# Attention phase of a two-layer gated cross-attention stack: weight codes made in the middle batches and read back in the last one

## The reference

```python
x = x + tanh(g_xattn[0]) * mha(layernorm(x), ctx, ctx, W_Q, b_Q, W_K, b_K, W_V, b_V, W_O, b_O)   # 16 heads of 32
x = x + tanh(g_ffn[0]) * bitlinear_ffn(layernorm(x), w_gate, w_up, w_down)    # inner width 2048
x = x + tanh(g_xattn[1]) * softmax_attention(layernorm(x), ctx)
x = x + tanh(g_ffn[1]) * (mxfp4(x, delta_act) @ mxfp4(weight, delta_w).T + bias)
# batch 8, 512 rows, width 512

def _weight_quant(w):                       # for w_gate, w_up, w_down
    scale = 1.0 / clip(mean(abs(w)), 1e-05)
    return clip(round(w * scale), -1.0, 1.0) / scale

def mxfp4(x, delta):                        # for the last weight, in blocks of 32
    scale = exp2(floor(log2(max(abs(x)))) - 2) * exp2(0.5 * tanh(4 * delta))
    return scale * sign(x) * fp4_round(clip(abs(x / scale), 0, 6))
```

## Time and profile before

| | us |
|---|---|
| median of 3 runs (lowest, highest) | 1665.71 (1661.42, 1668.95) |
| the profiled execution, its whole time | 1667.24 |
| its span, first to last instruction | 1665.5 |
| attention phase in it | 0 to about 891 |
| first exponential of the last batch | 760.2 |
| store of the last head group | 888.2 |
| mean granted TensorE clock, as a share of 2.4 GHz | 0.939 |

### The profile page before, as it was taken

How to read it: one execution, slowest core, us unless ns; L and a number is a source line. 1 busy time by engine, 2 the same in 40 slices (tenths; PEclk the granted TensorE clock), 3 DMA queues, 4 the chain that set the end, 5 groups by cost and what they waited for, 6 DMA issues and landing times. The chain is left out here.

```text
span 1665.5 us, 24701 instructions
## 1 busy us (share of the span) xinstructions
PE 1482.8 (89%) x6969; PEld 937.8 (56%) x6969; DVE 1237.6 (74%) x2141; ACT 875.0 (53%) x1434; POOL 922.8 (55%) x1160
## 2 busy tenths in 40 slices
PE   5799999899999999998654999999999838999996
PEld 3556556566655656665222555555555416888885
DVE  3567787978878777776653888888888707899996
ACT  4256566555555655645452555555555415555652
POOL 3167567567667657665473343344333115888874
PEclk9899999999999999998756999999999959999998
DMA  5836658394674838359654444444444362555531
GB/s 179 254 114 205 192 165 240 116 266 133 187 224 142 257 97 250 116 151 261 183 168 114 99 105 108 116 104 117 110 104 107 71 239 84 161 160 189 179 92 61
DMA packets 247452, 259.03 MB, mean 156 GB/s; under 512 B 140076, under 2 KB 156984, under 8 KB 243768
## 3 DMA queue, kind: packets, MB, share of 16 engines
q1 hardware_dynamic: 247352, 257.85, 53.9%
HBM read 149.50 MB, written 76.58 MB: 136 GB/s over the span
## 5 line engine op out<-in xcount | busy, mean ns | idle before, releaser
L660 ACT ACTIVATE a_probs<-a_sc 128x512 f32<-128x512 f32 x512 | 299.8, 595 | 298.5 <-PE a_sc L556 297.1
L745 DVE TENSOR_REDUCE a_negmax<-a_mx 128x1 f32<-128x512 f32 x512 | 337.6, 674 | 99.3 <-PE a_mx L539 98.3
L870 POOL TENSOR_TENSOR a_acc<-a_acc,a_probs 128x512 f32<-128x512 f32 x256 | 331.2, 1321 | 23.2 <-ACT a_probs L660 22.2
L870 POOL TENSOR_TENSOR a_acc<-a_probs 128x512 f32<-128x512 f32 x128 | 166.3, 1318 | 258.2 <-ACT a_probs L660 257.3
L539 PE MATMUL a_mx<-a_stack 96*128 96x512 f32 x512 | 230.8, 451 | 51.0 <-DVE a_negmax L745 38.7
L556 PE MATMUL a_sc<-a_stack 97*128 97x512 f32 x512 | 218.3, 429 | 26.7 <-ACT a_probs L660 19.2
L1020 PE MATMUL bank<-wcode,b_xq 128*128 128x512 bf16 x1024 | 228.0, 381 | 6.6 <-DMA b_xq<-b_xcode 6.6
L539 PEld LDWEIGHTS a_mx<-a_stack 96*128 96x128 f32 x512 | 101.8, 199 | 127.1 <-DVE a_negmax L745 76.4
L1020 PEld LDWEIGHTS bank<-wcode,b_xq 128*128 128x128 bf16 x1024 | 100.4, 98 | 129.2 <-DMA b_xq<-b_xcode 7.8
L751 DVE RECIPROCAL a_attn<-a_den 128x128 f32<-128x128 f32 x128 | 120.9, 948 | 59.7 <-PE a_den L584 59.7
L514 PE MATMUL a_work<-a_xt,k_wbuf 128*128 128x512 f32 x384 | 124.4, 439 | 13.0 <-DVE a_xt L722 13.0
(11 more groups left out here) (165 smaller groups left out, 2645.7 us busy)
## 6 DMA issues: line engine op xcount, KB each, us to landing
a_stack<-spill SPq DMA_DIRECT2D x192, 256.0 KB, 4.7
spill<-k_part SPq DMA_DIRECT2D x64, 512.0 KB, 3.5
ctx_t<-k_wo SPq DMA_DIRECT2D x16, 1024.0 KB, 7.9
c_ct<-ctx_t SPq DMA_DIRECT2D x7, 2048.0 KB, 8.2
a_stage<-in_x_dram SPq DMA_DIRECT2D x32, 256.0 KB, 5.0
a_stage<-in_ctx_dram SPq DMA_DIRECT2D x32, 256.0 KB, 2.7
attn_t<-a_attn SPq DMA_DIRECT2D x32, 256.0 KB, 4.4
b_xin<-in_x_dram SPq DMA_DIRECT2D x32, 256.0 KB, 2.7
```

Of the source, the lines that this page charges most:

```text
L660: nc.scalar.activation(probs[:, k, j, :], sc[i % 2][:], ACT.Exp, scale=SCALE).then_inc(exp_done, 1)
L745: nc.vector.tensor_reduce(negmax[:, g % 2, j, t:t + 1], mx[i % 2][:], axis=AX.X, op=ALU.max, negate=True).then_inc(mx_done, 1)
L870: nc.gpsimd.tensor_tensor(acc[:, j], probs[:, 0, j] if k == 1 else acc[:, j], probs[:, k, j], ALU.add)\
```

## The change

Three things move, all in `attention_phase`.

1. The last weight. It is loaded whole (1 MB) into `wsum` at the start, and its chain runs on VectorE in batch 0: steps 0 to 2 behind the last context transpose, steps 3 to 5 behind the second Q product's remainder, and four rounds of steps 6 to 11 between the first 20 `max` steps. One store writes it out. Batches 1 to 4 have no part of it any more.
2. The ternary weights. The sums are taken in 12 units of 128x2048 (two halves each) in groups 1 to 12, counted over all batches. From group 14 on, which is group 2 of batch 3, to group 25 (group 1 of batch 6), one unit a group is loaded, rounded in two halves (`uround`), clipped (`uclip`, `ucode`) and stored as codes to DRAM (`code_t`). The last batch only issues the twelve transposing DMAs, now from DRAM, and splits W_O.
3. The last batch's `pv` steps stand at ticks 74, 88, 112 and 142 (`pv_last`) in place of 128 to 149.

```diff
-    CH, SUMS, RAWS = 4, 8, 3
+    CH = 4
+    UNITS = 3 * CH
...
+    SUM_FIRST, CODE_FIRST, QSTEPS = 1, 14, 6 + 6 * C
...
-        raws = [nc.alloc_sbuf_tensor_at(f"raw{n}", [P, 2048], F32, offset=place["xt"] + 8192 * n)[:] for n in range(2)] + [wsum[:]]
-        codes = nc.alloc_sbuf_tensor_at("codes", [P, 2, 2048], BF16, offset=place["stage"])[:]
-        wraw, wmag = wsum[:, 1024:1024 + D], wsum[:, 1024 + D:1024 + 2 * D]
+        codes = nc.alloc_sbuf_tensor_at("codes", [P, 4, 1024], BF16, offset=place["wsum"])[:, :, 0:512]
+        wmag = probs[:, T - 1].rearrange("p j s -> p (j s)")
+
+        def unit(k):
+            per = wsrc[k // CH].shape[1] // CH
+            return per, wsrc[k // CH][:, k % CH * per:(k % CH + 1) * per, :]
...
-            ck.add(base + 20, 9, "sload", g)
-            ck.add(base + BURST + 2, 9, "sum", g)
-        ck.add(BURST + at["den"], 9, "wscale")
-        ck.add(-60, 9, "wload1")
-        for n in range(QSTEPS):
-            ck.add(PERIOD * (n // 6) + BURST + n % 6, 9, "wquant", n)
-        ck.add(2 * PERIOD + 30, 9, "wstore1")
-        for k, tick in enumerate(ITEM_AT):
-            ck.add(tick, 9, "rload", k)
-            for h in range(2):
-                ck.add(tick + 30 + 6 * h, 9, "rround", k, h)
-            ck.add(tick + 40, 9, "rclip", k)
-            ck.add(tick + 44, 9, "rcode", k)
-            ck.add(tick + 50, 9, "rturn", k)
+            ck.add(base + 60, 9, "uload", g)
+            ck.add(base + BURST + 2, 9, "sum", g, 0)
+            ck.add(base + BURST + 10, 9, "sum", g, 1)
+            ck.add(base + BURST + 2, 9, "uround", g, 0)
+            ck.add(base + BURST + 10, 9, "uround", g, 1)
+            ck.add(base + BURST + 12, 9, "uclip", g, 0)
+            ck.add(base + BURST + 20, 9, "uclip", g, 1)
+            ck.add(base + BURST + 29, 9, "ucode", g)
+            ck.add(base + BURST + 44, 9, "ustore", g)
+            for n, tick in enumerate((5, 35, 95)):
+                ck.add(base + tick, 9, "uturn", g, n)
+            for k, tick in enumerate((74, 88, 112, BURST + 14)):
+                ck.add(base + tick, 6, "pv_last", g, k)
+        ck.add(PERIOD + BURST + at["den"], 9, "wscale")
+        ck.add(PERIOD + 60, 9, "woload")
+        ck.add(PERIOD + BURST + 2, 9, "wohigh")
+        ck.add(PERIOD + BURST + 20, 9, "wolow")
...
                             load_small()
+                            sp.dma_start(wsum[:].rearrange("p (c e) -> p c e", c=C), weight.rearrange("(c p) e -> p c e", p=P))\
+                                .then_inc(q_loaded, 16)
...
+                    elif name == "uload":
+                        n = b * G + args[0]
+                        if n == SUM_FIRST:
+                            sp.wait_ge(q_step, QSTEPS)
+                            sp.dma_start(w1_code, wsum[:].rearrange("p (c e) -> p c e", c=C)).then_inc(q_stored, 16)
+                            sp.wait_ge(q_stored, 16)
+                        if SUM_FIRST <= n < SUM_FIRST + UNITS:
+                            k = n - SUM_FIRST
+                            if k:
+                                sp.wait_ge(summed, 2 * k)
+                            per, src = unit(k)
+                            sp.dma_start(wsum[:].rearrange("p (o i) -> p o i", o=per), src).then_inc(s_loaded, 16)
+                        if CODE_FIRST <= n < CODE_FIRST + UNITS:
+                            k = n - CODE_FIRST
+                            if k:
+                                sp.wait_ge(u_stored, 16 * k)
+                            else:
+                                sp.wait_ge(summed, 2 * UNITS)
+                            per, src = unit(k)
+                            sp.dma_start(wsum[:].rearrange("p (o i) -> p o i", o=per), src).then_inc(u_loaded, 16)
+                    elif name == "ustore" and CODE_FIRST <= b * G + args[0] < CODE_FIRST + UNITS:
+                        k = b * G + args[0] - CODE_FIRST
+                        sp.wait_ge(u_code, k + 1)
+                        sp.dma_start(code_t[k].rearrange("p (a n) -> p a n", a=4), codes).then_inc(u_stored, 16)
+                    elif name == "uturn" and b == NB - 1:
+                        k = args[0] * 3 + args[1]
                         if k == 0:
+                            sp.wait_ge(u_stored, 16 * UNITS)
                             sp.wait_ge(qk_full, 2 * G * NB)
+                        if k == 2 * CH:
                             sp.wait_ge(v_full, T * NB)
+                        sp.dma_start_transpose(wcode[:, k], code_t[k]).then_inc(u_turned, 16)
+                    elif name == "woload" and b == NB - 1:
+                        sp.wait_ge(u_stored, 16 * UNITS)
+                        sp.dma_start(wsum[:].rearrange("p (c e) -> p c e", c=C), w_o.rearrange("(c p) e -> p c e", p=P))\
+                            .then_inc(wo_loaded, 16)
...
-                    elif name == "pv":
+                    elif name in ("pv", "pv_last"):
                         g, k = args
+                        if (it + shift == NB - 1) != (name == "pv_last"):
+                            return
...
+                            if it + shift == 0 and g == 0 and k == T - 1:
+                                act.wait_ge(q_step, QSTEPS)
...
+                    elif name == "uround" and CODE_FIRST <= (it + shift) * G + args[0] < CODE_FIRST + UNITS:
+                        g, h = args
+                        k = (it + shift) * G + g - CODE_FIRST
+                        half = wsum[:, h * 1024:(h + 1) * 1024]
+                        if h == 0:
+                            act.wait_ge(u_loaded, 16 * (k + 1))
+                            if k == 0:
                                 act.wait_ge(w_scaled, 1)
+                        nc.scalar.activation(half, half, ACT.Copy, scale=scale_w[:, k // CH:k // CH + 1], bias=ROUND).then_inc(u_round, 1)
...
+                def quantise(n):
+                    c, step = (n - 6) // 6, n if n < 6 else 6 + (n - 6) % 6
+                    u, m = wsum[:], wmag
+                    if n >= 6:
+                        u, m = u[:, c * D:(c + 1) * D], m[:, c * D:(c + 1) * D]
+                    if n:
+                        dve.wait_ge(q_step, n)
...
+                        if it + shift == 0 and i == 2 * T - 1:
+                            dve.wait_ge(q_loaded, 16)
+                            for n in range(3):
+                                quantise(n)
...
+                        if it + shift == 0 and (g, side) == (1, Q):
+                            dve.wait_ge(exp2_done, 2)
+                            dve.wait_ge(gated, 1)
+                            for n in range(3, 6):
+                                quantise(n)
...
+                        slot_n = g * T * J + i - 1
+                        if it + shift == 0 and 0 <= slot_n < 5 * C:
+                            if slot_n % 5 == 0:
+                                quantise(6 + slot_n // 5 * 6)
+                            quantise(6 + slot_n // 5 * 6 + 1 + slot_n % 5)
...
+                    elif name == "uclip" and CODE_FIRST <= (it + shift) * G + args[0] < CODE_FIRST + UNITS:
+                        g, h = args
+                        k = (it + shift) * G + g - CODE_FIRST
+                        half = slice(h * 1024, (h + 1) * 1024)
+                        dve.wait_ge(u_round, 2 * k + h + 1)
+                        if h:
+                            dve.wait_ge(u_clip, 2 * k + 1)
+                        nc.vector.tensor_scalar(codes[:, 2 * h:2 * h + 2], wsum[:, half].rearrange("p (a n) -> p a n", a=2), ROUND, 1.0, ALU.subtract, ALU.min).then_inc(u_clip, 1)
+                    elif name == "ucode" and CODE_FIRST <= (it + shift) * G + args[0] < CODE_FIRST + UNITS:
+                        k = (it + shift) * G + args[0] - CODE_FIRST
+                        dve.wait_ge(u_clip, 2 * k + 2)
+                        nc.vector.tensor_scalar(codes, codes, -1.0, None, ALU.max).then_inc(u_code, 1)```

PE, last batch, group 2. `a_mx` and `a_sc` are the max and score products, `a_pvb` the V products, `a_den` first the turned maxima, then the sums. Before:

```order
L539 MATMUL a_mx<-a_stack 128x512 [waits a_mx_done]
L556 MATMUL a_sc<-a_stack 128x512 [waits a_exp_done] x3
L545 MATMUL a_den<-k_ident,a_negmax 16x128 [waits a_recip_done,a_mx_done]
L556 MATMUL a_sc<-a_stack 128x512 [waits a_exp_done]
L567 MATMUL a_pvb<-a_probs,a_v 32x512 [waits a_attn_done]
L567 MATMUL a_pvb<-a_probs,a_v 32x512 x11
L567 MATMUL a_pvb<-a_probs,a_v 32x512 [waits a_exp_done]
L567 MATMUL a_pvb<-a_probs,a_v 32x512 x3
L584 MATMUL a_den<-a_acc,a_ones 32x512 [waits a_mt_done,a_acc_done]
```

216 lines of the change are left out of this document (67 added, 149 removed).

## The result

| | before | after |
|---|---|---|
| median, us (7 runs each, side by side) | 1665.72 | 1677.88 |
| lowest, highest | 1661.42, 1668.95 | 1668.62, 1683.38 |
| ratio, 95% interval | | 1.0075 (1.0055 to 1.0094) |
| first exponential of all | 75.1 | 76.1 |
| first exponential of the last batch | 760.2 | 805.4 |

What follows compares the result with a forecast made beforehand. PE paces the middle batches; in the last, engines queue behind code items. Terms 7 + 2 - 7 + 3 + 6 - 30 = -19 took 1667.2 to 1648.2 profiled, 1647 as a median; range 1630 to 1664.

Steps and rivals of the forecast that it cites:

- Term E: Middle batches: a 1 MB load between spill and refill costs 1 us in six batches; +6 us, bounds 0 and +15.
- rival (3): 1 MB loads in 24 of 32 groups each delay something PE waits for; with 1.7 us each, 1682; chance with neighbours 0.09.
- F: Last batch: code items leave, POOL's sums are late next; 95.9 us against 128.0, -30 us, bounds -22 and -36.
- The V products: Last batch: moving them is worth little by itself; they fill PE's gaps and keep its clock up; no separate size.
- C: Third groups of batches 1 to 4: the last weight's chain leaves; -7 us, bounds -5 and -8.
- A: Batch 0: the last weight's chain comes in, steps 6 to 11 delay the last maximum; +7 us, bounds 0 and +12.
- B: Rest of batch 0: fourth round beside first scores, SP waiting for the weight's store, late first load; +2 us, bounds 0 and 3.
- D: Twelve middle groups: coding's rounding and clips in the burst cost 0.25 us a group; +3 us, bounds 0 and 12.
- Rival (1): The middle pays nothing: clips sit in the gap, refill not later; D = E = 0, A = 5, 1636; chance 0.17.
- signs of being wrong: Prediction wrong if middle batches grow by over 2 us each, or a last-batch group takes more than 26 us.

Runs made afterwards that it cites:

- late_g2: The changed kernel with the whole 1 MB load of each group 2 at tick 95, behind the refill, nothing split; one run, 1658.11 us.
- before_mrow: The kernel before with only the refill (2, K) moved to slot 47.5, so the row of maxima is issued ahead of it; 1656.71 us, ratio 0.9956.
- split_g2: The changed kernel with group 2's 1 MB load in halves, one before the spill (tick 45), one behind the refill (tick 95); 1653.88 us, ratio 0.9948.
- best: The changed kernel with group 2's load in halves (ticks 45, 95), refill (2, K) at slot 47.5, last batch's V products at old ticks; 1620.76 us, ratio 0.9751.
- best_nochain: As best, with the 24 steps 6 to 11 of the last weight's chain left out; 1618.75 us, ratio 0.9725.

## Why the prediction was wrong

**Term E is the step that failed**: "at some 300 GB/s the load takes 3.5 us, of which about 2.5 pass while SP waits for the spill. I take 1 us times 6". Measured it is some 47 us in place of 6 (of which about 1 is coding): 16 of wait and 12 of lower clock in third groups, and 19 in fourth ones. It failed in two places.

- The third groups. I let 2.5 of the 3.5 us pass unseen and put the bound at 2.5 a batch. The rows show 3.58 us of idle PE at 349.83 and up to 4.8, and the group grew by 3.7 to 6.9 in five batches and by 1.9 in the last. The load is not over when SP issues the refill; it lands 4.1 us later. And I put the clock at nothing here: in the five batches it fell to 0.88 to 0.94 in this group, and PE's own products took 1.5 to 2.9 us longer. The Trainium skill (DMA: Bandwidth & Descriptors, "Queues, rings and completion order") says that a DMA engine consumes descriptors in ring order, though a later one may finish its write first. The trace agrees with the order: the refill landed later with the load ahead of it, and the same load behind the refill (late_g2) cost under 0.3 us in five of the six batches. I had weighed that rule and set it aside for a guess about what passes during SP's wait, which no row of before could bear out.
- The fourth groups. The prediction had nothing for them ("refills of groups 1 to 3 show no wait on PE"). That sentence was true of the kernel before, and it looked at the wrong client. What waits there is not the refill but the row of maxima, one place behind it in SP's list. The rows were before me: the row made at 65.44 and issued at 70.26. I read them as slack ("SP had 4 us of slack"), when they were 5 us on the path at the start, as before_mrow shows; in the middle batches the same order was slack of about 2 us, and the loads used it up.

This is rival (3)'s mechanism, "the 1 MB loads", to which I gave 0.09. Its price was right in the mean and wrong in shape: 47 / 24 is 2.0 us a load where I had 1.7 for the slower case, but 12 of the 24 loads, in first and second groups, showed no wait of this kind, and 12 cost 3.9 each.

**F, the last batch: right in its number, in part by luck.** -32.9 against -30. With the V products at their old ticks F is -38, and moving them, which I put at almost nothing, cost 5: two misses of opposite sign. By groups 24.2, 23.1, 23.1 and 25.5 were worked out and 25.8, 22.3, 21.9 and 25.1 measured. That POOL's sums are late next holds as far as `den` stands right behind about 15 us of them; but they are not all that sets the end, since the batch changed by 5 us with the order of PE alone. The transposes from DRAM landed in 5.2 us in the middle where those from SBUF had taken 4.3, and no group of the last batch shows it.

**The V products: wrong sign.** "worth little by themselves", and "they fill PE's gaps and keep its clock up". The clock rose in the second group, and 5 us were lost. F without them is -38, beyond the bound of -36.

**C, the chain leaves: right.** Third groups of batches 1 and 2 are 23.6 and 23.5 us in split_g2 and 23.4 and 23.5 in best; 23.7 was forecast.

**A, the chain in batch 0: too large.** First exponential forecast at 82, measured 76.1. The last maximum of the first group did slip, from 64.1 to 68.5, near the +6 that I worked out; but of these 4.4 us the first exponential shows 1.0, or 1.4 to 2.2 if counted from the first maximum in the six kernels with this start, since SP issued the row only at 71.28 in after and at 70.26 before. With SP's stop gone the chain costs 2.5 (best_nochain). **B** can't be told from the rest.

**D, the coding: right within its bounds.** In best third groups without coding (batches 0 to 2) take 23.4 to 23.5 us and those with it (3 to 5) 23.6, 24.0 and 23.6; fourth groups 24.1 to 24.2 (batches 1 and 2) and 24.2. That is 0.3 and less than 0.1 us a group, and 0.25 was the term. The cost lies elsewhere, in first groups: those of batches 1 to 3 take 23.2 to 23.3 us and those of batches 4 and 5, with coding, 25.1 and 24.9, all at a clock of 1.00. In batch 5 of best the clips stand ahead of the first maximum of the group, which starts at 559.12, and a max product waits for it:

```profile
556.15 1.46 DVE L828 TENSOR_SCALAR codes<-a_wsum 128x1024 bf16<-128x1024 f32 x2
557.64 0.69 DVE L832 TENSOR_SCALAR codes<-codes 128x2048 bf16<-128x2048 bf16 x1
```

```profile
559.80 0.50 PE L546 MATMUL a_mx<-a_stack 96*128 96x512 f32 x1 [1.36 <-DVE a_negmax L788]
```

With 0.5 for batch 6 (24.3 against 23.8 before) that makes D about 5 where I had 3. No run left the coding out, so this is read from the rows and not tested. Second groups vary too much with the clock to tell. The prediction compared two different steps, 1505 ns while POOL adds and 410 when it is done. The same step tells the same: the chain's first clip of 512 columns, 1505 ns before, takes 419 ns in batch 0 after, where POOL is busy for a small part of the time. Twelve POOL additions of 1.3 us would be 15.6, not the +12 of the prediction. Rival (1), that the middle pays nothing, holds neither for D nor for E.

With E at zero the forecast would have been 1641. Best, where E is repaired, stands at 1620.76. Of the 20 us between, 8 are F's (-38 against -30) and 9 the first exponential (72.6 against 82), half of which was free in the kernel before. The upper bounds of the terms add up to +15, not to the +20 of the prediction; the measured +12 lies below both, with E alone at three times its bound. One of its signs of being wrong did show: middle batches were to grow by no more than 2 us, and batches 0 to 5 grew by 4.5 to 10.7 each.

## What to carry to other kernels

A bulk load should not stand in a queue between two DMAs of which the second is waited for: look for each transfer that an engine waits for and put the load behind it. A sequencer that waits for a landing holds back every DMA that stands behind it, so look what else is ready at that time, and let it go first. And a row that is "ready but issued 5 us later" is slack only if nobody waits for it; follow it to its reader before you call it so.

## What the runs showed of the hardware

- A refill of three DMAs of 256 KB was usable 5.2 us after its issue with no load ahead of it, and 7.5 us after it with 1 MB issued 3.0 us ahead. A load of 0.5 MB in the same place lengthened the group by 0.3 to 0.5 us in batches 0 to 2 (no coding), 1 MB by 3.7 to 5.5, of which 2.2 to 2.8 are idle time and the rest is a clock of 0.94 and 0.88.
- Moving one DMA issue by one place in SP's list gave the kernel before 7 us (0.9956, 0.9938 to 0.9974).
- Twelve V products moved in between the scores of each group of the last batch made it 5 us longer, in six kernels against three, though the clock was higher in its second group.
- First groups with PE busy throughout took 23.2 us at a granted clock of 1.00 and 24.8 at 0.93. What decides between the two was not settled, and of the differences between kernels some 5 us may be this.
